# Waits of the values' projection, square-root steps, softmax inverses and weight maxima in a retention, pooling and FFN kernel

## The reference, cut

```
x' = rotation of the feature pairs of x by angles frequencies * delta_t, with amplitudes ** delta_t
q, k, v = split(x' @ W_qkv.T), 16 heads of 16;  k = layernorm(k) over the head
S_t = gamma * S_(t-1) + v_t k_t^T;  y_t = S_t q_t        (16 x 16 state per head)
x1 = x + y @ W_o.T
scores = tanh(x1 @ W1 + b1) @ v;  p = softmax(scores under a mask by the sequence's kind)
pooled = (p @ x1) / count
out = x1 + FFN(pooled): 8-bit fake quantization of pooled, of w_gate, w_up (704 x 256), w_down (256 x 704)
      and of silu(gate) * up; a weight row's scale is max|row| / 127
```

## Time and profile before

| | us |
|---|---|
| median of 3 runs | 279.13 (278.16 to 279.15) |
| the profiled execution's own time | 279.3 |
| its span in the trace | 277.6 |

### The profile page before, as it was taken

The page is one execution under the profiler, slowest core; times in us unless marked ns, Lnnn a source line. Parts: engine busy times, 40 slices in busy tenths (PEclk is TensorE's granted clock), DMA queues, the critical chain, the costliest instruction groups (busy, mean ns, idle before and its releaser), DMA issues.

```text
span 277.6 us, 8491 instructions
## 1 busy us (share of the span) xinstructions
PE 255.3 (92%) x3545; PEld 176.0 (63%) x3545; DVE 232.6 (84%) x501; ACT 180.6 (65%) x316; POOL 145.2 (52%) x140
## 2 busy tenths in 40 slices
PE   5898999988998899899899999998889999998995
PEld 5767769657877777777777886885634434433331
DVE  4999869479699878978987786787888999999994
ACT  2775481552467647768748547527689999847991
POOL 6939595990593278059339533003212679850570
PEclk9999999999999999999999999999999999999999
DMA  5990504400900530194084033040009489000167
GB/s 164 336 275 3 153 0 151 159 2 13 293 5 2 190 117 2 35 291 43 0 302 62 2 129 84 2 138 22 0 0 200 113 219 348 35 0 0 72 256 280
DMA packets 30311, 31.20 MB, mean 112 GB/s; under 512 B 12929, under 2 KB 20673, under 8 KB 30273
## 3 DMA queue, kind: packets, MB, share of 16 engines
q1 hardware_dynamic: 30272, 30.66, 37.2%
HBM read 19.48 MB, written 8.42 MB: 100 GB/s over the span
## 4 chain that ended last, share of the span: by engine, by line
PE 45%; DVE 32%; ACT 13%; issue 6%; DMA 1%; POOL 1%; DVEq 0%; ACTq 0%
PE psum L879 11%; PE psum L1271 6%; PE psum L904 4%; DVE yT_lo L1480 4%; PE psum L1290 3%; DVE psum L1475 3%; PE psum L986 3%; ACT silu L842 2%; PE psum L961 2%; ACT silu L824 2%; PE psum L1030 2%; DVE arena L1468 2%; PE psum L942 2%; PE psum L1023 2%; DVE arena L1651 2%
## 5 line engine op out<-in xcount | busy, mean ns | idle before, releaser
L1460 DVE TENSOR_TENSOR arena<-psum,xq_mem 128x512 f32<-128x512 f32 x64 | 39.7, 682 | 7.0 <-PE psum L904 7.0
L531 POOL TENSOR_TENSOR xT_lo<-arena,xT 128x512 fp32r<-128x512 f32 x14 | 18.0, 1308 | 46.1 <-ACT xT L662 46.1
L1271 PE MATMUL psum<-xq_mem,guT 128*128 128x512 bf16 x152 | 33.9, 380 | 0.2
L662 ACT ACTIVATE xT<-arena 128x512 fp32r<-128x512 f32 x14 | 8.1, 623 | 29.5 <-PE psum L879 26.0
L1271 PEld LDWEIGHTS psum<-xq_mem,guT 128*128 128x128 bf16 x152 | 14.4, 98 | 19.4 <-DVE arena L1651 1.8
L1662 DVE TENSOR_REDUCE h_max<-arena 128x1 f32<-128x1024 f32 (+1 forms) x24 | 25.9, 1123 | 0.2
L824 ACT ACTIVATE silu<-psum,gu_x 128x1024 f32<-128x1024 f32 (+1 forms) x24 | 24.4, 1025 | 2.1 <-PE psum L1271 1.1
L879 PE MATMUL psum<-wT,xT 128*128 128x256 f32 x64 | 17.3, 293 | 4.8 <-DVE arena L1468 4.8
L1475 DVE SCALAR_TENSOR_TENSOR psum<-psum,pmask,arena 128x256 f32<-128x256 f32 x28 | 12.3, 485 | 10.0 <-ACT arena L651 10.0
L904 PE MATMUL psum<-arena 32*64 32x128 f32 x1024 | 19.3, 278 | 1.1 <-issue 1.1
L644 ACT ACTIVATE arena<-psum,pmask 128x512 f32<-128x512 f32 x32 | 20.1, 684 | 0.1
(11 more groups left out here) (251 smaller groups left out, 734.1 us busy)
## 6 DMA issues: line engine op xcount, KB each, us to landing
arena<-in_x SPq DMA_DIRECT2D x9, 512.0 KB, 3.8
x_dram<-arena SPq DMA_DIRECT2D x8, 512.0 KB, 4.1
pooled<-x_dram SPq DMA_DIRECT2D x8, 512.0 KB, 5.3
out<-pooled SPq DMA_DIRECT2D x15, 256.0 KB, 2.2
xin<-in_x_t SPq DMA_DIRECT2D x7, 512.0 KB, 4.5
cs_rows<-cs_dram SPq DMA_DIRECT2D x12, 256.0 KB, 5.2
pooled<-in_w_qkv_t SPq DMA_DIRECT2D x3, 256.0 KB, 4.9
pooled<-in_w_down SPq DMA_DIRECT2D x1, 704.0 KB, 7.4
```

Source lines behind the costliest of these rows:

```text
L531: pool.tensor_tensor(xT_lo[:, k, :], xrotT[:, k, :], xT[:, k, :].bitcast(F32), ALU.subtract).then_inc(xl_ok, 1)
L1271: mm = pe.matmul(in_order(o[:, 512 * half:512 * half + 512], 2 * n + half), gT[i][:, v, c, :], xq_rows(2 * n + half, c), start=(c == 0), s ...
L1460: dve.tensor_tensor(dec[:, c, r, :, :], bank[S_BANK[r]].rearrange("q (n k) -> q n k", n=PP), two_heads, ALU.mult).then_inc(dec_done, 1)
```

## The change

In project_v the wait for rs_ok stays ahead of the first half (j = 0, bank 0), and the wait for x1_done goes to the second half (j = 1, bank 1). newton(g + 1) of stages 1 to 6 is split: four steps between low_y(g, 0) and y_odd(g, 1), seven at the old place. For that, sums_turn(g + 1) of stages 1 to 6 goes ahead of the values of the second half on TensorE, and sums_copy to right behind the softmax sums; in stage 0 it goes ahead of low_y(0, 1). softmax_weights(c) is split: the sum stays, the product, the reciprocal and pn go into the next stage, between scale_v and decays(g, 1). The weights' maxima go to stages 1, 2 and 3, ahead of y_odd(g, 0), and their multiplications and reciprocals to stages 2, 3 and 4, behind the softmax inverse; the clip factors to stage 5, the same place.

```diff
--- before.py
+++ after.py
@@ -238,6 +238,7 @@
         ang_ok, trig_ok, pow_ok = sem("ang_ok"), sem("trig_ok"), sem("pow_ok")
         lg_abs, lg_exp, lg_one, lg_ln, lg_ok = (sem(n) for n in ("lg_abs", "lg_exp", "lg_one", "lg_ln", "lg_ok"))
         dec_arg, dec_exp = sem("dec_arg"), sem("dec_exp")
+        amax_ok = sem("amax_ok")
         g_sc_ok, d_sc_ok = [sem("gate_sc_ok"), sem("up_sc_ok")], sem("d_sc_ok")
         rot_c, rot_left, rot_half, rot_done = sem("rot_chain"), sem("rot_left"), sem("rot_half"), sem("rot_done")
         xT_tr, xT_ok = sem("xT_tr"), sem("xT_ok")
@@ -1064,12 +1065,11 @@
 
             def project_v(g):
                 pe.wait_ge(kT_ok, DC * g + DC)
-                if g:
-                    pe.wait_ge(rs_ok, g + 1)
-                    pe.wait_ge(x1_done, 2 * g - 1)
                 for j in (0, 1) if g else (1, 0):
-                    if g == 0 and j == 0:
-                        pe.wait_ge(rs_ok, 1)
+                    if j == 0:
+                        pe.wait_ge(rs_ok, g + 1)
+                    elif g:
+                        pe.wait_ge(x1_done, 2 * g - 1)
                     for p in range(2 * j, 2 * j + 2):
                         tokens = slice(p * P, p * P + P)
                         parts(V_BANK[j][:, (p % 2) * D:(p % 2) * D + D], DC, lambda k: xT[:, k, tokens], lambda k: xT_lo[:, k, tokens],
@@ -1171,11 +1171,11 @@
                     else:
                         pe.wait_ge(w1o_ok, 1)
                     project_whole(Q_BANK, 0, 0, q_mm)
+                    if g:
+                        sums_turn(g + 1)
                     values_pair(1, 0)
                     values_pair(1, 1)
-                    if g:
-                        sums_turn(g + 1)
-                    else:
+                    if g == 0:
                         squares(1, 1)
                     project_whole(Q_BANK, 0, 1, q_mm)
                     if g == 0:
@@ -1440,18 +1440,19 @@
             low_weights(1, raw_qkv[:, :, 2 * D:3 * D], wT[:, 2, :, :], wT_lo[:, 2, :, :])
 
 
-            def scales(raw, amax, inv, signal):
-                link(dve.tensor_reduce(amax, raw, AX.X, ALU.max, apply_absolute_value=True))
+            def gu_largest(i):
+                dve.wait_ge(ld_gu[i], 16 * 3)
+                dve.tensor_reduce(g_sc[:, i, :], raw_gu[i], AX.X, ALU.max, apply_absolute_value=True).then_inc(amax_ok, 1)
+
+            def down_largest():
+                dve.wait_ge(ld_d, 16)
+                dve.tensor_reduce(d_amax[:, 0, :], raw_d, AX.X, ALU.max, apply_absolute_value=True).then_inc(amax_ok, 1)
+
+            def scales(i, amax, inv, signal):
+                dve.wait_ge(amax_ok, i + 1)
                 link(dve.tensor_scalar(amax, amax, 1.0 / QMAX, None, ALU.mult))
                 dve.reciprocal(inv, amax).then_inc(signal, 1)
 
-            def gu_scales(i):
-                dve.wait_ge(ld_gu[i], 16 * 3)
-                scales(raw_gu[i], g_sc[:, i, :], g_inv[:, i, :], g_sc_ok[i])
-
-            def down_scales():
-                dve.wait_ge(ld_d, 16)
-                scales(raw_d, d_amax[:, 0, :], d_amax[:, 1, :], d_sc_ok)
             def decays(g, c):
                 for r in range(QR):
                     dve.wait_ge(s_mm, NS * g + QR * c + r + 1)
@@ -1496,8 +1497,8 @@
 
 
             N_LINKS = 1 + 3 * NEWTON
-            def newton(g):
-                done = [0]
+            def newton(g, part=None):
+                done = [0 if part != 1 else 4]
 
                 def step(ins):
                     done[0] += 1
@@ -1507,13 +1508,20 @@
                 def by_block(m):
                     return m.rearrange("q (n k) -> q n k", k=NH)
 
-                dve.wait_ge(var_mm, g + 1)
+                if part != 1:
+                    dve.wait_ge(var_mm, g + 1)
                 t, seed = (by_block(scratch[:, 4 + i, :]) for i in range(2))
                 y = by_block(rs[:, :])
                 ve = sq_cols.rearrange("q (n k) -> q n k", k=32)[:, :, 0:NH]
-                step(dve.tensor_scalar(seed.bitcast(I32), ve.bitcast(I32), 1, None, ALU.logical_shift_right))
-                step(dve.tensor_scalar(y.bitcast(I32), seed.bitcast(I32), -1.0, RSQRT_SEED, ALU.mult, ALU.add))
-                for n in range(NEWTON):
+                if part != 1:
+                    step(dve.tensor_scalar(seed.bitcast(I32), ve.bitcast(I32), 1, None, ALU.logical_shift_right))
+                    step(dve.tensor_scalar(y.bitcast(I32), seed.bitcast(I32), -1.0, RSQRT_SEED, ALU.mult, ALU.add))
+                    step(dve.tensor_tensor(t, ve, y, ALU.mult))
+                    step(dve.scalar_tensor_tensor(t, t, -0.5, y, ALU.mult, ALU.mult))
+                if part == 0:
+                    return
+                step(dve.scalar_tensor_tensor(y, t, 1.5, y, ALU.add, ALU.mult))
+                for n in range(1, NEWTON):
                     step(dve.tensor_tensor(t, ve, y, ALU.mult))
                     step(dve.scalar_tensor_tensor(t, t, -0.5, y, ALU.mult, ALU.mult))
                     last = dve.scalar_tensor_tensor(y, t, 1.5, y, ALU.add, ALU.mult)
@@ -1542,9 +1550,12 @@
                 dve.tensor_tensor(sm[:, :, :], rows, sm_c[:, 0, :].unsqueeze(2).to_broadcast([P, PP, S]),
                                   ALU.subtract).then_inc(s_sub, 1)
 
+            def softmax_sums(c):
+                dve.wait_ge(ex_ok, c + 1)
+                dve.tensor_reduce(sm_c[:, 1, :], ex[:, :, :], AX.X, ALU.add).then_inc(cond_c, 1)
+
             def softmax_weights(c):
-                dve.wait_ge(ex_ok, c + 1)
-                cstep(c, 3, dve.tensor_reduce(sm_c[:, 1, :], ex[:, :, :], AX.X, ALU.add))
+                dve.wait_ge(cond_c, C_LINKS * c + 3)
                 cstep(c, 4, dve.tensor_tensor(sm_c[:, 2, :], sm_c[:, 1, :], cnt[:, PP * c:PP * c + PP], ALU.mult))
                 if c >= TURNED:
                     cstep(c, 5, dve.reciprocal(inv_sum[:, c % 2, :], sm_c[:, 2, :]))
@@ -1568,6 +1579,18 @@
                 decays(g, 0)
                 for p in range(PP) if g else (2, 3, 0, 1):
                     scale_v(g, p)
+                if 2 <= g < G - 1:
+                    softmax_weights(c - 1)
+                if 2 <= g < 4:
+                    scales(g - 2, g_sc[:, g - 2, :], g_inv[:, g - 2, :], g_sc_ok[g - 2])
+                elif g == 4:
+                    scales(2, d_amax[:, 0, :], d_amax[:, 1, :], d_sc_ok)
+                elif g == 5:
+                    dve.wait_ge(lg_exp, 2)
+                    link(dve.tensor_scalar(clip_s[:, 1, :], clip_s[:, 0, :], 1.0, QMAX, ALU.add, ALU.mult))
+                    link(dve.reciprocal(clip_s[:, 2, :], clip_s[:, 1, :]))
+                elif g == G - 1:
+                    softmax_weights(c - 1)
                 decays(g, 1)
                 if g == 0:
                     dve.wait_ge(w1o_mm, 1)
@@ -1580,31 +1603,29 @@
                     largest_rows(c - 1)
                 if g == G - 1:
                     y_odd(g, 0)
-                if g:
+                    softmax_sums(c)
                     softmax_weights(c)
-                if g == G - 1:
                     low_y(g, 0)
-                if g < G - 1:
+                elif g:
+                    softmax_sums(c)
+                    sums_copy(g + 1)
+                    if g < 3:
+                        gu_largest(g - 1)
+                    elif g == 3:
+                        down_largest()
                     y_odd(g, 0)
-                    if g:
-                        sums_copy(g + 1)
                     low_y(g, 0)
-                if g == 3:
-                    gu_scales(1)
-                elif g == 4:
-                    down_scales()
-                elif g == 2:
-                    gu_scales(0)
-                    dve.wait_ge(lg_exp, 2)
-                    link(dve.tensor_scalar(clip_s[:, 1, :], clip_s[:, 0, :], 1.0, QMAX, ALU.add, ALU.mult))
-                    link(dve.reciprocal(clip_s[:, 2, :], clip_s[:, 1, :]))
+                    newton(g + 1, 0)
+                else:
+                    y_odd(g, 0)
+                    low_y(g, 0)
                 y_odd(g, 1)
+                if g == 0:
+                    sums_copy(1)
                 if g < G - 1:
                     low_y(g, 1)
-                if g == 0:
-                    sums_copy(1)
                 if g + 1 < G:
-                    newton(g + 1)
+                    newton(g + 1, 1 if g else None)
                 else:
                     dve.wait_ge(pl_mm, G - 1)
                     for b in range(2):
```

## The result

The changed kernel takes 278.79 us (median of 20 executions), the kernel before 279.74 in the same comparison: a ratio of 0.9952 [0.993, 0.9973], by which it is 1.3 us less (the medians differ by 0.95). The forecast was 278.3 us with 274.6 to 280.0 as its range.

What follows compares the result with a forecast made beforehand. TensorE, busy 92% of the span, was taken as the bound, with gains only where it stands still. Terms -7.4 + 0.8 + 3.45 + 1.15 + 1.15 = -0.85 us took the median 279.13 to 278.3 us, range 274.6 to 280.0.

Steps and rivals of the forecast that it cites:

- The six residual waits: TensorE's waits for residual(g-1, 0) before the values' projection, stages 2 to 7: all gone, -5.15 us.
- Rival 4: project_v's first half still waits, rs_ok being the last signal; 0.5 us back in three stages, 279.8 us; chance 0.08.
- The sums: TensorE's transpose of the squares' sums no longer waits for sums_copy: -0.8 us in stage 0, -1.45 in stage 1.
- yT: Second-half output projection waits 1.15, 0.6, 0.45 us in stages 1 to 3, maxima being ahead of y_odd(g, 0); together +0.8.
- pn: weights_turn, stages 2 and 3: TensorE waits 1.7 us each for pn, blocked behind GpSimd's L531; +3.45 us.
- Stage 4: The values wait for decays(4, 1), late because VectorE's tensor_scalar is blocked behind the second L531; +1.15 us.
- Stage 5: GpSimd's L531 starts before VectorE's product, so the values wait as in stage 4; +1.15 us.
- rival 1: VectorE starts ahead of GpSimd in stage 5, one wait of 1.15 us less: 277.1 us; chance 0.24.
- Rivals 2 and 3: 2: little is blocked beside GpSimd, 273.3 to 275.6 us, chance 0.20; 3: root steps hold y_odd(g, 1), 281.3, 0.08.

Runs made afterwards that it cites:

- The wait edit alone: Kernel before with only project_v changed: first half waits for rs_ok alone, second for x1_done; 277.75 us, ratio 0.992.
- the gate: Changed kernel with GpSimd's low_x waiting for VectorE's pn in stages 2 and 3, for the w_down scales in stage 4; 273.11 us, ratio 0.9757.
- gate in stage 4: Changed kernel with GpSimd's low_x made to wait for the w_down scales in stage 4 alone; 276.25 us, ratio 0.988.
- The better version: Changed kernel with low_x waiting in stages 2 to 4 and the three weight maxima moved into idle stretches of VectorE; 270.68 us, ratio 0.9673.
- the moves undone: Changed kernel with inverses, maxima, scales and clip factors back in their old stages and places, split wait and split roots kept; 276.87 us, ratio 0.9882.
- race: Changed kernel with one more small VectorE reduction ahead of the product in stage 5 alone; 279.47 us, ratio 0.9962.
- pn back: Changed kernel with the softmax inverses and pn back ahead of sums_copy in stages 1 and 2; 277.64 us, ratio 0.9922.

## Why the prediction came out as it did

- **The six residual waits, -5.15.** Right. T to v is 4.11 us in every stage from 1 to 7; the six stages lost 29.67 - 24.66 = 5.0 us.
- **Rival 4, that rs_ok would take the wait's place.** It doesn't in the changed kernel, and does in the two kernels with the roots in one run, 0.5 us in three and in four stages. The wait edit alone takes 2.9 us off T to v, all the edits without the split (with the gate) take 3.4, the changed kernel 5.0. So most of the step is the split's.
- **The sums, -0.8 and -1.45.** Right as far as shown: -0.85 at T of stage 1, and no wait before L1064 in stage 1.
- **yT, waits of 1.15, 0.6 and 0.45.** The right three places, measured 0.9, 0.4 and 0.3, which with 0.07 each for the restart is 0.4 us less in all. That is a part of why T of stage 4 is 0.2 ahead of the forecast. (The prediction's 0.71 + 0.28 + 1.74 is 2.73, not 2.65; measured, y_odd of stage 1 starts 58.68 - 56.19 = 2.5 us behind the squares, since the records overlap.)
- **pn, 2 x 1.7.** Right: a wait of 1.63 in each of the two stages, -3.4 us when the gate took both away. VectorE came at v + 1.2 instead of v + 1.5; since it then waits for GpSimd, whose start is fixed, that changed nothing.
- **Stage 4, 1.15.** Right: a wait of 1.0, and 1.1 us by its own gate.
- **Stage 5, 1.15, the step that failed.** Out of 1.03 for VectorE and 0.97 for GpSimd the prediction took GpSimd to be first. VectorE started at v + 0.94, GpSimd at v + 0.97. The argument that stood under rival 1, the next instruction's start before the last one's recorded end, was the better one: scale_v's record goes to 140.91, the product starts at 140.83. Nor is it a coin that falls anew each time: in all seven traces in which nothing delays VectorE in stage 5 the product is 0.02 or 0.03 us ahead. The rival's 277.1 us is nearly what the 12 executions from 277.25 to 277.6 took.
- **Why the median lies at 278.8 and not there.** Of the changed kernel's 32 executions 11 had a mean clock below 0.99 and took over 280 us, and a few lie between. The prediction had no term for that. Without it the forecast would have been 1 us too high; its nearness to the median is in part two errors against each other, and so in part luck. The start it was counted from moved too: 279.13 by three runs, 279.74 in the comparison. As differences, -0.85 was forecast, and -1.3 measured by the ratio.
- **Rivals 2 and 3** didn't happen. Everything predicted as blocked was blocked, except the product of stage 5; and yT is waited for less than forecast, not more.

What the whole shows: 7.3 us were taken off TensorE's path (5.0 + 2.25), and by v of stage 7 only 2.0 of them are left. The other 5.3 came back as new waits, of which 4.3 are for small VectorE operations, each of 0.15 to 0.42 us when nothing is in its way.

## What to carry to other kernels

A small operation that is moved into a gap costs what the engine beside it makes of it: look up in the trace which GpSimd instruction runs at the new place, and whether the operation's longest instance is several times its shortest. If so, either put an operation there that keeps its time beside GpSimd (here a maximum), or let GpSimd wait until the small operations are through, where GpSimd has idle time. And measure the parts of a change by themselves: here two moved waits gave 2.2 us, all the edits together 1.3, all of them with four lines on GpSimd 6.8, and with the maxima in idle time too 9.2 (by the ratios). The better version still leans on the 0.03 us of stage 5; a gate in that stage was not tried.

## What the runs showed of the hardware

- **Less than 0.2 us in the order of two starts decide over 1.1 us.** Stage 5 with VectorE 0.03 ahead: product 0.15 us. With it 0.16 behind: 1.14 us. With it 0.46 behind: 0.83.
- **VectorE gets in between two GpSimd instructions.** low_x is two instructions of 1.27 us back to back (2.49 together), yet the 128x4 product ends at 70.95, with the first, and the reciprocal runs beside the second in its usual 0.18.
- **GpSimd can be held too.** Behind pn, which it met in stage 1 with the moves undone, a GpSimd instruction of 0.61 us took 0.80; behind the shorter product none was seen to grow.
- **The granted clock fell in some executions of one kernel.** In the disturbed execution TensorE stood still from 94.6 to 96.25, at weights_turn in stage 3. The stretches behind it (us; busy time of PE, PEld, DVE, ACT, POOL, each with its count; granted clock of TensorE; DMA share; GB/s):

```profile
94.00:95.00 1.00, 0.63 (x41) 0.38 (x31) 0.93 (x3) 0.84 (x2) 1.00 (x2) 1.00 0.98 371
95.00:96.00 1.00, 0.00 (x0) 0.00 (x0) 1.00 (x1) 0.00 (x0) 0.91 (x1) 1.00 0.55 201
96.00:97.00 1.00, 0.75 (x4) 0.44 (x6) 0.97 (x5) 0.27 (x1) 0.00 (x0) 0.86 0.95 293
...
98.00:106.00 8.00, 8.00 (x80) 6.41 (x77) 3.49 (x7) 1.98 (x4) 7.76 (x8) 0.50 0.02 6
...
107.00:108.00 1.00, 1.00 (x6) 0.82 (x5) 0.00 (x0) 0.84 (x2) 0.85 (x2) 1.00 0.00 0
```

  Full clock (2.4 GHz) through the idle time, then, from within the microsecond in which work resumes, half of it (1.2) for ten microseconds of a busy TensorE, and back. In this execution it cost 4.6 us: from low_x of stage 2 to that of stage 4 it is 53.51 us, where the other trace has 48.91. Of the kernels with the two pn waits of 1.6 us (changed, race, gate in stage 4) 13 of 43 executions had a mean clock below 0.99, of all others whose clock is on record 1 of 93. Yet the gate in stage 4 had none in its 5, where some were expected, nor the kernels with single waits of 1.9 and 1.8 us (pn back, moves undone) in 10 and 4. And the race's trace has a shorter fall ahead of any pn wait, to 0.50 from 24 to 26 us. So idle time of that length goes with the long falls but isn't shown to be their cause or enough for them; what else is needed stays open.
